# One transpose per head for query and key, one pass for the row statistics, three slots instead of one, and a new order at both ends

## The reference, cut to what matters

```python
# x: (4, 2048, 256); 4 heads of 64
q, k = (split_heads(x @ w.T) * 64 ** -0.25 for w in (wq, wk))
v = split_heads(x @ wv.T)
q, k = rope(q), rope(k)                    # pairs of columns rotated by position
attn = softmax(q k^T + causal mask)
x = layernorm(x + (attn v) @ wo.T)
# feed-forward: a router, 32 experts, 16 adapters
ri = concat(x, [mean, std, min, max, l2, share of |x| < 1e-6])
h = gelu(ri @ r1_w.T + r1_b); probs = softmax(h @ r2_w.T)
x = layernorm(x + experts_and_adapters(x, probs))
```

## Time and profile before

| what | value |
|---|---|
| three runs, us | 2255.43, 2268.77, 2268.81 (median 2268.77) |
| the profiled execution: time, span, us | 2260.15, 2258.3 |
| PE, DVE, ACT, POOL busy, share of the span | 86%, 60%, 46%, 34% |
| mean granted PE clock | 0.911 of full speed |

### The profile page before, as it was taken

The page is one execution under the profiler, slowest core; times in us unless marked ns, Lnnn a source line. Parts: engine busy times, 40 slices in busy tenths (PEclk is TensorE's granted clock), DMA queues, the critical chain, the costliest instruction groups (busy, mean ns, idle before and its releaser), DMA issues. The chain is left out here.

```text
span 2258.3 us, 39106 instructions
## 1 busy us (share of the span) xinstructions
PE 1936.1 (86%) x13154; PEld 1727.6 (76%) x13154; DVE 1347.9 (60%) x3015; ACT 1040.6 (46%) x2293; POOL 775.0 (34%) x901
## 2 busy tenths in 40 slices
PE   5999999999999999999999999442178999999990
PEld 4778888878788878888878888341178999999980
DVE  7466554566654566554466663386885656656645
ACT  4344344444344444344444333315175666666655
POOL 1322043331043322033332000100085766766742
PEclk8799999999999999899999999555588999999995
DMA  4222122322223232222322221300004444554428
GB/s 121 69 75 76 47 73 70 90 76 78 60 73 78 77 84 75 62 61 61 90 80 83 64 66 27 139 34 0 0 14 128 137 156 141 155 172 133 143 50 298
DMA packets 154370, 198.48 MB, mean 88 GB/s; under 512 B 24612, under 2 KB 119824, under 8 KB 150124
## 3 DMA queue, kind: packets, MB, share of 16 engines
q1 hardware_dynamic: 138348, 186.33, 26.6%
q0 software_dynamic: 15872, 10.24, 2.7%
HBM read 129.65 MB, written 56.62 MB: 82 GB/s over the span
## 5 line engine op out<-in xcount | busy, mean ns | idle before, releaser
L518 PEld LDWEIGHTS out_ps<-v_sb,probs 128*128 128x128 f32 x4352 | 575.9, 197 | 30.6 <-ACT probs L642 7.3
L518 PE MATMUL out_ps<-v_sb,probs 128*128 128x65 f32 x4352 | 586.1, 275 | 3.6 <-ACT probs L642 3.3
L742 DVE TENSOR_REDUCE part_max<-rows_ps 128x1 f32<-128x512 f32 (+2 forms) x576 | 345.5, 617 | 204.1 <-PE rows_ps L474 137.0
L642 ACT ACTIVATE probs<-scores_ps 128x512 f32<-128x512 f32 (+3 forms) x640 | 329.7, 533 | 146.9 <-PE scores_ps L505 74.8
L1502 PE MATMUL up_ps<-xe_t,w 128*128 128x320 f32 x1920 | 289.8, 311 | 1.7 <-DVE xe_t L1609 1.7
L1502 PEld LDWEIGHTS up_ps<-xe_t,w 128*128 128x128 f32 x1920 | 284.6, 189 | 2.4 <-issue 1.9
L501 PE MATMUL scores_ps<-q,k_st 128*128 128x512 f32 (+2 forms) x640 | 279.3, 436 | 0.0
L474 PE MATMUL rows_ps<-k_st,q 128*128 128x512 f32 (+3 forms) x640 | 246.3, 408 | 25.3 <-DVE part_max L742 15.3
L896 POOL TENSOR_TENSOR products<-qk,cos_sin 128x256 f32<-128x256 f32 x224 | 160.2, 747 | 280.3 <-ACT qk L599 280.3
L502 PE MATMUL scores_ps<-q,k 68*128 68x512 f32 (+2 forms) x640 | 238.7, 373 | 0.0
L1465 POOL DMA_INDIRECT acc_rows<-out_rows,token x96 | 148.7, 1549 | 127.5 <-ACT out_rows L1592 116.5
(11 more groups left out here) (243 smaller groups left out, 2960.8 us busy)
## 6 DMA issues: line engine op xcount, KB each, us to landing
w_raw<-in_w_expert SPq DMA_DIRECT2D x32, 1536.0 KB, 6.5
k<-k_st SPq DMA_DIRECT2D x160, 128.0 KB, 2.3
q<-q_up_cols SPq DMA_DIRECT2D x128, 128.0 KB, 2.8
w_raw<-in_w_adapter SPq DMA_DIRECT2D x32, 384.0 KB, 7.1
x_t<-in_x_t SPq DMA_DIRECT2D x64, 128.0 KB, 2.3
q_up_cols<-q_st SPq DMA_DIRECT2D x64, 128.0 KB, 2.4
q_low_cols<-q_st SPq DMA_DIRECT2D x64, 128.0 KB, 2.5
x_row<-in_x SPq DMA_DIRECT2D x64, 128.0 KB, 2.1
```

The lines of the kernel that those rows point to most:

```text
L518: mm = pe.matmul(o_ps[:, u % 2, s * (HD + 1):(s + 1) * (HD + 1)], probs[:, g % P_RING, s * P:(s + 1) * P], v_sb[:, place(b, j), h, :], sta ...
L642: act.activation(probs[:, g % P_RING, low:CH], s_ps[:, g % S_RING, low:CH], ACT.Exp).then_inc(exp_done, 1)
L742: red = dve.tensor_reduce(to, r_ps[:, e % 2, 0:width], AX.X, ALU.max, negate=g == 0)
```

## The change

- `w_qkv` is reordered so that the 64 query and 64 key columns of a head lie side by side. One transpose per head turns both; `dup`, `qt` and `kt` become one step `turn` at three slots after `v`. ACT copies one upper part, DVE subtracts one lower part (`parts`, a ring of two). SP stores query parts to memory as before and, new, copies the key's upper and lower half from `parts` into `k_st` (two more transfers for each tile); whoever reads the key waits for those transfers (`keys_stored`).
- The statistics are written three times, at columns 0, 32 and 64 of a 96-wide block; the three products of upper and lower parts are then one contraction over 96 rows. POOL makes the two copies.
- `x1` comes three slots after `wo`; `stats` one slot after `x1`; the rest of it is a step of its own, `sparse`, one slot later. `y`, `x1`, `rstd`, `moments` get four buffers, `attn_t` two.
- First tiles: rotations of tiles 1, 4 and 7 on POOL, projections up to two tiles ahead; only unit 0's maxima come before slot 0, those of units 1 to 3 are dealt to slots 0 to 8; `load_q` of the first four units is issued before the last stores.
- Last four tiles: started one slot apart, each PSUM step with the next of six banks.

```diff
+FIRST_ON_POOL = (1, 4, 7)
...
     for n, e in enumerate(early):     # early: maxima and turns of units 0 to 3
         u = e[1]
+        if u == 0:
+            before.append(e)
+        else:
+            at = (0, 0, 0, 0, 2, 2, 3, 3, 5, 5, 6, 6)[n - GROUP] if e[0] == "max" else (1, 4, 8)[u - 1]
+            stream[at].append(e)
...
-        apart = 2 if i // GROUP == len(groups) - 1 else 7
+        apart = 1 if i // GROUP == len(groups) - 1 else 7
...
-                                  ("dup", 3, False), ("qt", 1, True), ("kt", 1, True)))
+                                  ("turn", 3, True)))
...
-        steps = (("ot", 0, True), ("wo", 2, True), ("x1", 2, False), ("stats", 0, False), ("x1t", 2, True))
+        steps = (("ot", 0, True), ("wo", 2, True), ("x1", 3, False), ("stats", 1, False), ("sparse", 1, False),
+                 ("x1t", 2, True))
...
+    def store_qk(n):
+        sp.wait_ge(qk_lower, n + 1)
...
         for part_, to in enumerate(("q_up", "q_low")):
             sp.dma_start(dram[to][...], raw(parts[0:HD, n % 2, part_])).then_inc(qk_stored[n % 2], 16)
+        for part_ in range(2):
+            sp.dma_start(raw(k_st[part_ * HD:(part_ + 1) * HD, :, cols(n)]),
+                         raw(parts[HD:P, n % 2, part_])).then_inc(qk_stored[n % 2], 16)
...
     def load_k2(q):
-        sp.wait_ge(k_upper, b * NT + GROUP * (c + 1))
+        keys_stored(sp, b * NT + GROUP * (c + 1) - 1)
...
+            for u in range(HEADS):
+                load_q(u)
+                load_k2(u)
+                if u < 2:
+                    store_qk(FIRST - 2 + u)
...
     def turn_heads(out, n):
+        pe.wait_ge(*at_banks(roped_ready, n))
         for h in range(HEADS):
             mm = pe.transpose(out[:, h * P:(h + 1) * P],
-                              roped[:, r, first + h].rearrange("p a b c -> p (a b c)"), ident[:])
+                              roped[:, n % 2, 2 * h:2 * h + 2].rearrange("p a b c -> p (a b c)"), ident[:])
...
-                    three(out, lambda a: w_r1s[:, a, :], lambda b: x1_ts[:, b].rearrange("p a b -> p (a b)"),
-                          start=False).then_inc(hid_done, 1)
+                    pe.matmul(out, w_r1s[:], x1_ts[:].rearrange("p a b -> p (a b)"), start=False, stop=True)
...
+            def copy_turned(out_ps, n):                 # ACT
+                act.wait_ge(qk_turned, n + 1)
                 if n >= 2:
+                    act.wait_ge(qk_stored[n % 2], 64 * (n // 2))
+                act.copy(parts[:, n % 2, 0], out_ps.rearrange("p (h d) -> p h d", h=HEADS))
...
+                elif kind == "sparse":                  # POOL
                     pool.wait_ge(moments_ready, k + 1)
                     pool.wait_ge(abs_ready, k + 1)
+                    pool.tensor_tensor(x1[:, k % ROW_RING, D + 1:D + 5:3], powers_of[:], power[:, 1:3], ALU.pow)
+                    pool.wait_ge(powers_ready, k + 1)
+                    pool.tensor_copy(blocks[:, 1:], blocks[:, 0:1].to_broadcast([P, STAT_BLOCKS - 1, NSTAT]))\
+                        .then_inc(stats_ready, 1)
```

More of the change, by code:

```diff
@@ L93, in attention_plan @@
         begins[u] = max(slot, -1)
+    early = [("max", u, 0, s) for u in range(HEADS) for s in range(GROUP)] + [("turn", u) for u in range(HEADS)]
+    stream = [[e for e in now if e not in early] for now in stream]
     before = stream.pop(0)
-    before.sort(key=lambda e: (e[1], e[0]))
+    assert not before
+    for n, e in enumerate(early):
+        u = e[1]
+        if u == 0:
[3 more added lines that the diff above has]
+            stream[at].append(e)
+            begins[u] = min(begins[u], at)
+    for now in stream:
+        now.sort(key=lambda e: e[1])
     ends = [first[HEADS * (k + 1)] for k in range(len(groups))]
@@ L131, in attention_plan @@
         if kind in after:
-            earlier += [x for x in [(after[kind], n - 1)] if x in every]
+            other, back = after[kind]
+            earlier += [x for x in [(other, n - back)] if x in every]
         if any(x not in made for x in earlier):
@@ L137, in attention_plan @@
         b, t = n // NT, n % NT
-        if kind in ("v", "kt") and t >= 8 and b:
+        if kind in ("v", "turn") and t >= 8 and b:
             at = max(at, ends[4 * b - 1])
-        while claims and at in taken:
+        while claims and at in taken and at < total:
             at += 1
@@ L151, in attention_plan @@
         side.pop()
-    return groups, units, chunks, first, before, stream, begins, side, made
+    bank_of, used, claimed = {}, [0, 0], {kind for _, _, steps in chains for kind, _, claims in steps if claims}
+    for g, now in enumerate(side):
+        for kind, n in now:
+            if kind in claimed:
+                late = g >= total
+                bank_of[kind, n] = used[late] % (M_RING + S_RING + R_RING if late else M_RING)
+                used[late] += 1
+    return groups, units, chunks, first, before, stream, begins, side, made, bank_of
 def attention(nc, dram, NB, NT):
-    groups, units, chunks, first, before, stream, begins, side, made = attention_plan(NB, NT)
+    groups, units, chunks, first, before, stream, begins, side, made, bank_of = attention_plan(NB, NT)
     CHUNKS = len(chunks)
@@ L445, in _, with claim @@
             pe.wait_ge(v_copied, FIRST)
[L446 to L455, removed]
+            pe.wait_ge(qk_lower, FIRST)
+            holder = [None] * len(banks)
+            def claim(kind, k, semaphore, value):
+                n = bank_of[kind, k]
+                if holder[n] is not None:
+                    pe.wait_ge(*holder[n])
+                holder[n] = (semaphore, value)
+                return banks[n]
             keys_seen, values_seen = [FIRST], [FIRST]
@@ L585, in _ @@
             walk(main, step)
-            pe.wait_ge(*holder[0])
+            for last in holder:
+                if last is not None:
+                    pe.wait_ge(*last)
         @block.scalar
```

386 lines of the change are left out of this document (205 added, 181 removed).

## The result

The changed kernel takes 2158.83 us (median of four runs, 2158.60 to 2158.95), the kernel before 2262.10 us in four runs beside it (2252.80 to 2268.81): ratio 0.9546, 95% interval 0.9502 to 0.9590. The forecast was 2154, range 2120 to 2210.

A forecast was written before the change was run, and what follows sets the result against it. PE was taken to bound the slots. Gains of 100 us there, 6 in first tiles and 4 in last tiles make 110; 2260 - 110 = 2150, with half of 8.6 put back for the median 2154 us, range 2120 to 2210.

The forecast's parts named there:

- Transposes: Slots: four fewer transposes in each of 56 tiles, 0.45 us per four on PE's path, 25 us gained.
- Statistics: Slots: two of three passes over statistics, 0.54 us together, fall away for each of 30 pairs, 11 us gained.
- DVE's block: Slots: cutting DVE's 2.4 us block in three takes 25 of 31.7 us of stalls and 26 of 32 us of dips.
- if dips follow stalls that aren't behind `x1`: Slots, sign in the changed kernel's profile: seeing this would mean the prediction was wrong on what makes the clock dips.
- Claims and ACT: Slots: fewer holders of `misc_ps` give 10 us; with ACT's 3.3 us of waits for probabilities, 13 us gained.
- Key through SP: Slots: two more SP transfers per tile, covered by orders 5 to 8 slots ahead; cost 0, bounds 0 and 30 us.
- slower: Rival, slots: the key's way through SP's queue makes PE wait for keys or queries; 2359 us, chance 0.05.
- no change: Rival, slots: ACT and POOL come late at `turn` and `x1t`, 116 us come back; 2270 us, chance 0.05.
- The stalls only move: Rival, slots: three DVE pieces still make PE stand long enough for the clock to fall; 2208 us, chance 0.16.
- First tiles: Start of the kernel: SP's five issues, 3 us per tile, decide; net 6 us gained, bounds -4 and 14.
- The step on the fifth unit's query: First tiles: its load, behind 26 issues, lands near 60 us, and PE waits for it in slot 1.
- Last tiles: After the slots: `sparse` about 3.1 us per tile, the first near 1427 by walking DVE's list; net 4 us, bounds 1 and 10.

The follow-up runs named there:

- e3: Changed kernel with the four transposes of `turn` made twice into the same place in the slots' 56 tiles: 2183.28 us.
- e2: Kernel before with only DVE's block dealt out: `x1` with its moments, `stats` a slot later, `sparse` another slot later: 2200.69 us, ratio 0.9732.
- e1: Changed kernel with `x1`, `stats` and `sparse` of a tile put back in one slot, nothing else undone: 2233.73 us.
- e13: Changed kernel with DVE's work in two pieces, `x1` and `stats` in one slot and `sparse` a slot later: 2183.17 us.
- e5: Changed kernel with each key and query store of a first tile issued one load of `x_t` later: 2155.94 us.
- e6: Changed kernel with POOL's wait for `weights_loaded` moved behind its first splits of `x_t`: 2157.70 us.
- e9: Changed kernel with rings of two for `powers_of`, `absolute`, `squares`, `junk`, and ACT waiting for `stats_ready` one tile earlier: 2157.00 us.
- e12: Changed kernel turning each tile of the slots a second time as its own step, with claim, ACT's copy and DVE's lower part: 2200.50 us.
- e10: Changed kernel with first-tile stores one load later and all eight rotations on DVE, so POOL waits for no weights: 2147.30 us.

## Why the prediction was right, and where it was not

*Transposes*: 25 forecast, 24.5 in e3 (1.7 of it perhaps a dip). The distance between two weight loads was the right price, as PE is the bound.

*Statistics*: 11 forecast, 18.6 by rows. The step "A third of it each gives 0.36" took the 0.54 us for three passes and nothing else; a pass is 0.12 us, and the rest is a gap behind the passes over 6 rows. There is a like gap ahead of them, which the step left out, and both went with the 6 rows. That the wider transpose costs nothing holds: it is followed after 0.11 us (340.89 to 341.00).

*DVE's block*: 25 for stalls and 26 for dips, 51; e2 measures 57.9 in the slots. The stalls fell by 28 and the dips to one of 3.4 us. The step was too careful, and what it says under the rivals, "stalls of 1.2 us and less show no dip in the trace", was true of that trace and false as a rule: in e1 and e13 waits of 1.04 and 1.13 us are followed by dips, in e5, e6 and e9 one of 0.8. Nor does a long stall always bring one: in the trace of before three of 1.8 to 2.1 us (479.31, 691.14, 1172.76) have none behind them, which the prediction doesn't say. By its own sign ("if dips follow stalls that aren't behind `x1`") it was wrong on what makes them: e3 has one behind a wait for POOL's `x_t_parts`, e12 one behind a claim. In the changed kernel no wait in the slots is over 0.8 us but one of 1.34, for `x_t_parts` at 111.71, with no dip behind it; e1, e3 and e13 have a dip of 3.4 us behind the same wait, so that the clock of 1.00 is in part luck.

*Claims and ACT*: 13 forecast. The slots gained 102.3; less 57.9, 24.5 and 18.6 leaves 1. The waits that the term named did go: those for `q_st` and `k_st` from 20.9 us to 5.6 (now for `parts`), those for `probs` altogether. But e2 has 9.4 and 3.3 of this without the merged step, so most of the term stands in the 57.9 already. e12, which adds a step with a claim to the changed kernel, gives 17, half of it a dip. The two don't agree, and what a claim alone is worth stays open. So the 100 us of the slots came out by errors that cancel: block and claims together had 64 and gave 59, the statistics had 11 and gave 18.6. POOL at `x1t`, taken as nothing within -5 and +8, fell from 5.3 to 1.4 us.

*Key through SP*: nothing in the slots, as forecast. The rivals "slower" and "no change" find no row: no wait for a transfer, and POOL's sums are never waited for at `turn`. "The stalls only move" is out by the 23.5 us.

*First tiles*: the step that failed by most. +6 forecast, -6.6 measured, 12.6 us of error. "What decides is SP ... so the last lower part is stored from about 44 us on" counted SP's five issues as a rate of 3 us for each tile. It missed that one of the five, the load of `x_t`, closes a ring through ACT, whose copy of the turned heads stands behind the cast of that load in ACT's order; the ring takes 6.6 us, three times. It also let the rotations on two engines pass as a part of the cost and not as a pace, and did not see that POOL's wait for `weights_loaded` holds its first split, so that PE starts at 10.71 and not at 8.19. And "Eight maxima and two turns that stood before slot 0" is a miscount: by the two plans it is eleven maxima and one turn that move into the slots. With the first three undone (e10) the last lower part comes at 43.37, as forecast, and the first part gains 7.6 us over before by unit 0 (77.7 to 70.1) and 6.2 by the end of unit 3. The step on the fifth unit's query named a true wait: 4.79 us, at 74.47 instead of 60.

*Last tiles*: 4 forecast, 5.3 measured. The ring of `sparse`, POOL and ACT is there (e9), with 2.6, 3.8 and 3.8 us from one `sparse` to the next and not 3.1; the first comes 12.6 us after unit 63 where the walk had 16. No run undoes the banks or the new starts alone, so what each of them gave is not shown.

The half of 8.6 us put back for the median was hardly needed: the changed kernel's runs lie within 0.4 us, and the median of before came out 2 us above its profiled execution.

## What to carry to other kernels

Where one engine is the bound and another feeds it between blocks of its own work, cut those blocks and deal them out: here that alone gave 61 us, half of it through the clock. Price a group of passes from the load before it to the load behind it, or a gap at its edges is missed. Of a step added to an in-order queue ask not only its rate but which ring it closes: follow it from the queue through every engine that waits for what stands behind it, back to the queue. Where two causes share a pace, undoing one shows little; undo both before you drop either.

## What the runs showed of the hardware

The granted clock fell to half behind waits of PE as short as 0.80 us. In e5 (the wait in the timeline, and the busy time behind it; e6 and e9 have the same):

```profile
928.27 1.12 PE L474 MATMUL misc_ps<-ident,roped 128*128 128x128 f32 x4 [0.80 <-DVE attn_t L835]
```
```profile
928.20:931.60 3.40, 3.33 (x12) 2.94 (x13) 2.69 (x8) 1.08 (x2) 0.21 (x1) 0.50 0.01 2
```

In the changed kernel the same wait left the clock at full:

```profile
932.43 0.66 PE L473 MATMUL misc_ps<-ident,roped 128*128 128x128 f32 x4 [0.81 <-DVE attn_t L834]
```
```profile
932.40:935.80 3.40, 3.37 (x21) 2.82 (x21) 3.15 (x8) 1.08 (x2) 0.71 (x1) 1.00 0.04 9
```

In e1 it fell behind 1.04 us and stayed there for some 30 us, in which PE was hardly idle (the wait, and the busy time of the 40 us around it):

```profile
867.10 0.44 PE L622 MATMUL misc_ps<-ident,x 128*128 128x128 f32 x2 [1.04 <-DVE attn_t L834]
```
```profile
864.00:904.00 40.00, 38.76 (x180) 34.17 (x179) 19.07 (x53) 10.99 (x31) 2.90 (x6) 0.62 0.19 57
```

A wait of 1.68 us in the same run (455.37) was followed by none, and dips last from 3 to some 30 us. So the length of a wait does not tell what it costs; what else decides stays open.

Passes over 6 rows and over 96 rows both follow each other after 0.11 to 0.12 us. Between passes over 128 rows and passes over 6 rows PE lost 0.2 us each way (0.32 us from load to load in place of 0.12), and nothing between 128 and 96 rows. That the number of rows is the reason is not shown by a run of its own.
